# Feed-forward border of a one-core perceiver block: codes of h by two ScalarE additions, a W2 rounding moved behind the row maximum, four tiles turned early

## What is computed

```python
def _linear8bit(x, W, b):
    col_max = jnp.max(jnp.abs(x), axis=...)      # per column
    outlier = col_max > 3.0
    x_in = jnp.where(outlier, 0.0, x)
    x_out = jnp.where(outlier, x, 0.0)
    y = _ste_quant_rows(x_in) @ _ste_quant_rows(W).T
    return y + x_out @ W.T + b
h = _linear8bit(x, W1, b1)        # 256 x 4096
return _linear8bit(h, W2, b2)     # 256 x 1024
```

## Time and profile before

| | us |
|---|---|
| median of three executions | 937.74 (936.55 to 938.53) |
| profiled execution, device time | 937.01 |
| its span, first to last instruction | 934.9 |
| W1 stage's last matmul starts | 794.70 |
| W2 stage's first matmul starts | 803.87 |

### The profile page before, as it was taken

How to read it: one execution, slowest core, us unless ns; L and a number is a source line. 1 busy time by engine, 2 the same in 40 slices (tenths; PEclk the granted TensorE clock), 3 DMA queues, 4 the chain that set the end, 5 groups by cost and what they waited for, 6 DMA issues and landing times.

```text
span 934.9 us, 19043 instructions
## 1 busy us (share of the span) xinstructions
PE 897.1 (96%) x6856; PEld 820.6 (88%) x6856; DVE 702.4 (75%) x1124; ACT 614.1 (66%) x1060; POOL 488.2 (52%) x334
## 2 busy tenths in 40 slices
PE   7999999999999999999999999998899999799997
PEld 6997888888887889999999999986789999699997
DVE  6446666768546568888888888987988889988864
ACT  5424444565536478888888888885777878466662
POOL 0220000145444798686877868772377666266673
PEclk9999999999999999999999999999999999899999
DMA  8566766778763978656556565546135242224221
GB/s 320 191 206 232 290 224 250 277 271 308 278 189 113 271 224 271 199 183 183 182 176 215 172 193 169 195 168 215 46 136 181 97 172 94 87 91 180 90 90 46
DMA packets 80696, 174.82 MB, mean 187 GB/s; under 512 B 7632, under 2 KB 57584, under 8 KB 78064
## 3 DMA queue, kind: packets, MB, share of 16 engines
q1 hardware_dynamic: 79920, 173.63, 54.1%
q10 hardware_dynamic: 704, 0.23, 0.1%
HBM read 161.51 MB, written 11.53 MB: 185 GB/s over the span
## 4 chain that ended last, share of the span: by engine, by line
PE 73%; DVE 7%; issue 3%; ACT 3%; POOL 3%; DMA 2%; DVEq 0%; SPq 0%; ACTq 0%; POOLq 0%
PE bank L51 17%; PE bank L53 17%; PE bank L52 17%; PE bank L1408 4%; PE bank L1409 3%; PE bank L549 3%; PE bank L1379 3%; PE bank L1821 2%; PE bank L2051 2%; PE bank L1424 2%; POOL W_all L2287 1%; DMA ring<-in_L_attn_Wq_rope_dram 1%; ACT ring L1870 1%; DVE hT L1942 1%; POOL wl L1003 1%
## 5 line engine op out<-in xcount | busy, mean ns | idle before, releaser
L1003 POOL TENSOR_TENSOR wl<-ring,wh 128x1024 fp32r<-128x1024 f32 x68 | 161.6, 2395 | 0.0
L51 PE MATMUL bank<-act_all,W_all 128*128 128x256 f32 (+1 forms) x512 | 155.5, 304 | 3.0 <-POOL W_all L2287 2.0
L51 PE MATMUL bank<-act_all,wh 128*128 128x256 f32 x512 | 145.3, 284 | 1.8 <-POOL wl L1003 1.4
L53 PE MATMUL bank<-act_all,W_all 128*128 128x256 f32 (+1 forms) x512 | 145.4, 284 | 0.0
L52 PE MATMUL bank<-act_all,wh 128*128 128x256 f32 x512 | 144.7, 283 | 0.0
L53 PE MATMUL bank<-act_all,wl 128*128 128x256 f32 x512 | 144.3, 282 | 0.0
L513 POOL TENSOR_TENSOR xa_WT_l<-ring,xa_WT_h 128x1024 fp32r<-128x1024 f32 x16 | 43.5, 2741 | 176.6 <-ACT xa_WT_h L508 166.7
L1616 DVE TENSOR_TENSOR pl<-bank,ph 128x512 f16<-128x512 f32 x128 | 88.1, 688 | 47.1 <-ACT ph L1555 44.3
L2287 POOL TENSOR_TENSOR W_all<-rnd,W_all 128x512 fp32r<-128x512 f32 x72 | 92.1, 1289 | 54.5 <-ACT W_all L2176 54.4
L1000 POOL CAST wh<-ring 128x1024 fp32r<-128x1024 f32 x68 | 68.7, 1040 | 71.8 <-PE bank L53 66.0
L51 PEld LDWEIGHTS bank<-act_all,W_all 128*128 128x128 f32 x512 | 97.8, 191 | 4.4 <-POOL W_all L2287 2.6
(11 more groups left out here) (272 smaller groups left out, 2601.1 us busy)
## 6 DMA issues: line engine op xcount, KB each, us to landing
ring<-in_ctx_dram SPq DMA_DIRECT2D x16, 2048.0 KB, 7.9
ring<-in_L_attn_Wq_rope_dram SPq DMA_DIRECT2D x32, 1024.0 KB, 6.3
ring<-in_L_ffn_W_dram SPq DMA_DIRECT2D x14, 2048.0 KB, 7.6
panel<-in_L_ffn_W_dram SPq DMA_DIRECT2D x48, 512.0 KB, 4.3
w1p<-in_L_ffn_W_dram SPq DMA_DIRECT2D x16, 512.0 KB, 4.3
ring<-in_L_xattn_Wq_dram SPq DMA_DIRECT2D x2, 2048.0 KB, 12.8
ring<-in_L_xattn_Wk_dram SPq DMA_DIRECT2D x2, 2048.0 KB, 7.9
ring<-in_L_attn_Wo_dram SPq DMA_DIRECT2D x4, 1024.0 KB, 5.2
```

The lines of the kernel that those rows point to most:

```text
L51: pe.matmul(out, lh, rh, start=start, stop=False, skip_group_check=True)
L53: return pe.matmul(out, ll, rh, start=False, stop=stop, skip_group_check=True)
L1003: pool.tensor_tensor(half_of(l, i), half_of(r, i), f32(half_of(h, i)), ALU.subtract).then_inc(w_lo, 1)
```

## The change

- **Codes of h.** `codes` on DVE goes. ACT adds `mag2` to the scaled tile in place (`shifted_h`), then makes the high part by adding `-mag2` (`unmag2`, made once by ACT). DVE's `low_h` becomes a three-operand instruction that subtracts `mag2` and the high part. `shifted_h` stands in the even steps, `high_h` moves to the odd ones.
- **W2 rounding.** The rounding of tile 7 of the first W2 chunk, in the W1 stage's last step, moves behind the last `rows`; its high part on ACT moves too. Its low part is waited for only at k = 7 of step 0.
- **Turns.** Tiles 0 to 3 of chunk 1 are turned before step 0: 0 to 2 ahead of the row maximum's turn, 3 behind it. Step 0 then turns tiles 4 to 7 at k = 4 to 7, and step 1 none at k = 0 to 3. DVE rounds, and ACT takes the high part of, all eight tiles of chunk 1 in step 0.
- **PSUM.** The first two `scaled` read the inverse factors from the bank; the copy comes behind them. `clear(5)` moves into step 0.
- **Warm matmuls.** 5, 2 and 4 matmuls on zeros are put between PE's border steps.

```diff
@@ ffn2_tensor
-                pe.wait_ge(h_scaled, CH + NF)
-                for a in (6, 7):
-                    clear(a)
-                pe.wait_ge(r_max, NF + 1)
-                turn_rowmax(pe, runmax)
-                spread_factors(pe, 1)
-                pe.wait_ge(sx_copied, 2)
-                clear(4)
-                pe.wait_ge(q2_chain, 3)
-                clear(5)
-                pe.wait_ge(b_ready, 4 + (NW1 + 1) * KT)
-                pe.wait_ge(b_lo, 4 + (NW1 + 1) * KT)
-                pe.wait_ge(t_ready, (NW1 + 2) * CH)
...
                 def turn(c1, b, k):
                     pe.wait_ge(j_rnd, c1 * KT + (k + 1))
...
-                        if k < KT - LAG:
-                            if not first:
+                        if first == 0 and k >= KT - LAG:
+                            turn(1, 1, k)
+                        elif k < KT - LAG:
+                            if first is None:
                                 turn(c, b, k + LAG)
...
+                        if first == 0 and k == 0:
+                            pe.wait_ge(b_lo, 4 + (NW1 + 1) * KT - 1)
+                        elif first == 0 and k == KT - 1:
+                            pe.wait_ge(b_lo, 4 + (NW1 + 1) * KT)
...
+                            if first == 0 and k == 0 and j == 2:
+                                pe.wait_ge(q2_chain, 5)
+                                clear(5)
...
+                def warm(count):
+
+                    for _ in range(count):
+                        clear(7)
+
+                pe.wait_ge(h_scaled, CH + NF - 1)
+                clear(6)
+                pe.wait_ge(t_ready, (NW1 + 2) * CH)
+                for k in range(3):
+                    pe.wait_ge(b_ready, 4 + NW1 * KT + (4 + k + 1))
+                    turn(1, 1, k)
+                pe.wait_ge(h_scaled, CH + NF)
+                warm(5)
+                pe.wait_ge(r_max, NF + 1)
+                turn_rowmax(pe, runmax)
+                pe.wait_ge(b_ready, 4 + (NW1 + 1) * KT)
+                turn(1, 1, 3)
+                warm(2)
+                spread_factors(pe, 1)
+                pe.wait_ge(sx_copied, 2)
+                clear(4)
+                warm(4)
@@ ffn2_scalar
+                def shifted_h(nq, k, count=4):
+
+                    n = nq * KT + k
+                    tile = hT[:, ds(n, 1), :].rearrange("p a q -> p (a q)")
+                    act.wait_ge(q2_chain, n + count)
+                    act.activation(tile, tile, ACT.Identity, bias=mag2[:, ds(n, 1)]).then_inc(q2_b, 1)
...
-                                   hT[:, ds(n, 1), :].rearrange("p a q -> p (a q)"), ACT.Copy).then_inc(q2_hi, 1)
+                                   hT[:, ds(n, 1), :].rearrange("p a q -> p (a q)"), ACT.Identity,
+                                   bias=unmag2[:, ds(n, 1)]).then_inc(q2_hi, 1)
...
+                act.wait_ge(hm, (NW1 - 1) * 3 + 3 * CH)
+                act.activation(unmag2[:, :], mag2[:, :], ACT.Copy, scale=-1.0).then_inc(unmag_ready, 1)
+                act.wait_ge(b_ready, 4 + (NW1 + 1) * KT)
+                act.activation(W_h[0][:, KT - 1, :], rnd[(KT - 1) % 4][:, :], ACT.Copy).then_inc(b_hi, 1)
                 copy_factor(act, 1, sx2)
-                for k in range(KT):
-                    high_h(0, k)
...
+                for k in range(KT + 1):
+                    if k < KT:
+                        shifted_h(0, k, 3 if k < 2 else 4)
+                    if k >= 1:
+                        high_h(0, k - 1)
...
+                        if more and b == 1:
+                            high_h(nq + 1, k)
+                        if first == 0:
+                            high(1, k)
+                        elif k < KT - LAG:
+                            if first is None:
                                 high(c, k + LAG)
                         elif ahead:
                             high(c + 1, k + LAG - KT)
-                        if more:
-                            high_h(nq + 1, k)
+                        if more and b == 0:
+                            shifted_h(nq + 1, k)
                             for j in EVEN_AT[k]:
                                 scale_rows(c + 2, 0, n1 + 1, j)
@@ ffn2_vector
-                copy_inverse(dve, link, 1)
-                dve.wait_ge(b_lo, 4 + (NW1 + 1) * KT)
...
-                    dve.tensor_scalar(tile(hT, n), tile(hT, n), m, m, ALU.add, ALU.subtract).then_inc(q2_b, 1)
...
-                    dve.tensor_tensor(tile(hq_l, n), tile(hT, n), f32(tile(hq_h, n)), ALU.subtract).then_inc(q2_lo, 1)
+                    dve.scalar_tensor_tensor(out=tile(hq_l, n), in0=tile(hT, n), scalar=mag2[:, ds(n, 1)],
+                                             in1=f32(tile(hq_h, n)), op0=ALU.subtract, op1=ALU.subtract).then_inc(q2_lo, 1)
...
+                dve.wait_ge(row_spread, 2)
+                for k in range(2):
+                    scaled(k, bank[5][:, 0:T])
+                dve.tensor_copy(rsx[:, :], bank[5][:, 0:T]).then_inc(q2_chain, 1)
+                dve.wait_ge(q2_chain, 5)
+                for k in range(2, KT + 2):
                     if k < KT:
-                        scaled(k)
...
+                        scaled(k, rsx[:, :])
+                    low_h(k - 2)
+                dve.wait_ge(b_lo, 4 + (NW1 + 1) * KT)
...
+                        if first == 0:
+                            rounded(1, k, 0)
...
-                            scaled(nq * KT + (KT + k))
-                            codes(nq * KT + (KT + k))
+                            scaled(nq * KT + (KT + k), rsx[:, :])
@@ the W1 stage's last step: ACT, then DVE
-                            high(c + 1, 1 - b, k)
+                            if not (end and k == KT - 1):
+                                high(c + 1, 1 - b, k)
...
-                            rounded(c + 1, k, mag)
+                            if not (end and k == KT - 1):
+                                rounded(c + 1, k, mag)
...
+                        if end:
+                            rounded(c + 1, KT - 1, mag)
```

More of the change, by code:

```diff
@@ L1822, in turn, with step @@
                     last.then_inc(j_ready, 1)
-                def step(c, b, nq, ahead, first=False):
+                def step(c, b, nq, ahead, first=None):
                     for k in range(KT):
-                        if k < KT - LAG:
-                            if not first:
+                        if first == 0 and k >= KT - LAG:
+                            turn(1, 1, k)
+                        elif k < KT - LAG:
+                            if first is None:
                                 turn(c, b, k + LAG)
@@ L1855, in rows_back @@
                     last.then_inc(y_turned, 1)
-                step(0, 0, 0, True, first=True)
-                step(1, 1, 0, True)
+                def warm(count):
[18 more added lines that the diff above has]
+                warm(4)
+                step(0, 0, 0, True, first=0)
+                step(1, 1, 0, True, first=1)
                 with pe.Fori(1, NQ - 1) as i:
@@ L1907, in step @@
                             scale_rows(c + 1, 0, n1, k + 1)
[L1909 to L1910 removed]
+                step(0, 0, USE_W2, 0, True, first=0)
+                step(1, 1, USE_W2 + 1, 0, True, first=1)
                 with act.Fori(1, NQ - 1) as i:
                     for b in range(2):
[L1913 removed]
+                        step(i * 2 + b, b, i + (USE_W2 + b), i, True)
                 step(NCH - 2, 0, USE_W2 + NQ - 1, None, False)
@@ L1958, in rounded, with step @@
                     dve.tensor_scalar(rnd[k % 4][:, :], bank[k % 4][:, :], m, m, ALU.add, ALU.subtract).then_inc(j_rnd, 1)
-                for k in range(KT + 2):
-                    if k < KT:
-                        scaled(k)
-                    if 1 <= k < KT + 1:
-                        codes(k - 1)
-                    if k >= 2:
-                        low_h(k - 2)
-                def step(c, b, nq, ahead, more, first=False):
+                dve.wait_ge(row_spread, 2)
[4 more added lines that the diff above has]
+                for k in range(2, KT + 2):
+                    if k < KT:
+                        scaled(k, rsx[:, :])
+                    low_h(k - 2)
+                dve.wait_ge(b_lo, 4 + (NW1 + 1) * KT)
+                def step(c, b, nq, ahead, more, first=None):
                     for k in range(KT):
-                        if k < KT - LAG:
-                            if not first:
+                        if first == 0:
+                            rounded(1, k, 0)
+                        elif k < KT - LAG:
+                            if first is None:
                                 rounded(c, k + LAG, nq)
@@ L2184, in biased, with step @@
                         act.activation(tile, tile, ACT.Identity, bias=b1c[:, ds(n, 1)])
-                    def step(c, b, n2, inverse, first=False, tiles=TILES_AT):
+                    def step(c, b, n2, inverse, first=False, tiles=TILES_AT, end=False):
                         act.wait_ge(hp_ready, c * CH + CH)
```

(5 more changed lines are left out.)

27 lines of the change are left out of this document (9 added, 18 removed).

## The result

The changed kernel took 932.44 us, median of six runs (930.82 to 935.19), the kernel before 938.0 beside it: ratio 0.9939, 95% interval [0.9924, 0.9954]. That is 5.6 us faster. The forecast was 935.2 with a range of 932.0 to 939.2. The profiled execution took 932.16, its span is 930.1 (before 934.9), so 4.8 us of the gain can be looked for in the two traces.

The account below looks back on a forecast made before the run. PE, busy 96%, was taken as the bound, so gains come only where it waits or does needless work. Gains of 0.9 + 1.6 = 2.5 from profiled 937.0 give 934.5; median 0.7 above, 935.2; range 932.0 to 939.2.

Parts of the forecast that it names:

- The border: Between the last W1 and first W2 matmul: spread factors readable 0.95 us later; bounds 0.25 and 2.0 later.
- R: Time at the border when the spread factors can be read: 801.19 before, forecast 802.15 after.
- the zero matmul at 0.25: At the border, each matmul on zeros was costed at 0.25 us, five at 1.25.
- The bound of 2.0 later: Border's slow bound: count raised only after the moved rounding has ended, or transposes at half clock.
- Steps 0 and 1: Start of W2, up to the turn of chunk 2's tile 0: 827.15 instead of 828.04, 0.9 us earlier.
- last rounding R + 18.5: DVE's last rounding of step 0 starts 18.5 us after the spread factors can be read.
- the turn at R + 25.0: Chunk 2's tile 0 is turned in step 1, 25.0 us after the spread factors can be read.
- the 1.5 per pair: Step 0 on DVE: each `rounded` and `scaled` pair takes 1.5 us, about every second `scaled` held by POOL.
- Steps 2 to 5: W2 loop: each of two pairs of steps gives 0.8 us, 1.6 in all; bounds 2.9 won, 2.6 lost.
- w = 0.6: ACT's waits per pair of steps 2 to 5, taken as 0.6 us, so PE stands 0.9.
- Rival 2: ACT becomes the bound in W2's steps: w stays 2.75, four steps lose 2.6, total 940.1; chance 0.11.
- Rival 3: PE's clock falls in step 1 after standing 3 us: some 16 matmuls cost 1.5 more, 936.7; chance 0.12.

Follow-up runs that it names:

- the fifth experiment: The changed kernel with the codes of h back on DVE and `high_h` back in the even steps, other edits kept: 941.27 us, ratio 1.0035.

## Why the prediction was right, and where it was not

**The total** was right in its direction and range for a reason of which four fifths were not in it, and that is luck. The forecast won 2.5 us by the edits; they won about 1.1, less than the 1.9 that the forecast called the least difference to be told from none. With the tile's place undone the time was 937.35, also in the range and 2.15 above the 935.2, as the changed kernel is 2.8 below it. The other 4.5 came from the line that allocates `unmag2`, which the prediction didn't cost at all: it took a new small tile for nothing. No row of before shows that cost, since it is in each matmul's distance to the next, and nothing in the kernel before tells that this distance could be shorter.

**The border.** The mechanism on PE was right: the count comes just behind the last `runmax`'s start, PE's turns stand behind it and ahead of the row maximum's. On DVE, one of two terms was right: the `runmax` ahead of the last one takes 0.48 now, not the 1.27 that it took beside POOL's low part. The other failed: tile 3 of `hT` was to start 0.25 earlier, and it starts 0.97 behind the last W1 matmul, where it was 0.72, since DVE is busy until then with the `runmax` of the tile before. The last `runmax` starts 3.22 behind that matmul, not 2.7. From that `runmax` to R the steps give 802.15 - 797.4 = 4.75; measured 4.78 where the clock stayed up, 6.15 in the changed kernel's profile. The term that failed is the zero matmul at 0.25: five took 2.3 at half clock, 1.05 more, and the turn and its spread the rest. So R came 2.9 later against the last W1 matmul: 0.95 as forecast, 1.4 for the most part by the clock, 0.5 on DVE. The bound of 2.0 later had half clock for the transposes alone and was overrun by 0.9. Some of that is the profile of before, whose border was short: from the last `runmax` to R it took 2.77, but 3.30 in all four of its shifted forms.

PE waited 3.01 for L1966, a semaphore instruction of DVE with nothing to wait for itself. It ran at 793.6, behind the semaphore instructions of the last `runmax` (L2366, 793.4) and of the moved rounding (L2344, 793.5), but 0.26 ahead of the start of that rounding (793.86), which stands directly ahead of it in DVE's order. The Trainium skill's Perfetto Trace Analysis (Sequencer Loop) has engine instructions pushed into a queue, while the sequencer itself starts a control instruction. The trace agrees for the rounding, which waited only for its engine; the last `runmax`, whose wait was met late, was not passed.

**Steps 0 and 1.** First rounding at R + 8.0 as said, 8.06 measured; last rounding R + 18.5, measured 818.22, R + 18.6; the turn at R + 25.0, measured R + 25.05, and 25.05 to 25.10 in every kernel with these steps. The first W2 matmul at R + 2.3 was 2.5. These are the best terms of the forecast, but the 1.5 per pair is right only as a mean: `scaled` was to take 0.41 or 1.53 by turns, and it took 0.42, 1.34 and then 0.78 to 0.96 each time. What was wrong is what they were held against. Before's profile has the turn at R + 26.85; four kernels with the same code and other places have it at R + 25.73 to R + 25.75. The 1.1 is one instruction, the `scaled` of 1.53 in the earlier trace rows. In the kernel with the 256-byte tile, DVE's timeline has the same instruction as

```profile
822.83 0.42 DVE L1943 TENSOR_TENSOR hT<-hT,rows_q 128x256 f32<-128x256 f32 x1
```

and POOL's has its low parts as

```profile
822.78 2.91 POOL L1926 TENSOR_TENSOR W_all<-rnd,W_all 128x512 fp32r<-128x512 f32 x2 [2.25 <-ACT W_all L1877]
```

Each time POOL's instruction starts 0.05 ahead; once DVE's was held, once not. The Trainium skill's SBUF — State Buffer (SBUF: two separate sides) has the shared port pair as an exclusive lock, held by whichever starts first for the whole instruction. That fits the two lengths; the profile's starts, 0.05 apart, don't tell which came first. Where DVE's took 0.42, POOL's two took 2.90 to 2.92, and 2.73 where it took 1.53; this is as if POOL had waited instead, but no run shows it directly. So the true gain of these steps is 0.7 less what the border loses, where I had 0.9 after it.

**Steps 2 to 5.** Predicted 1.6, measured 2.35: the four distances at k = 4 make 10.81 before and 8.40 after, less 4 x 1.860 and 4 x 1.846. The other kernels without the edits make 11.06 to 11.24, the others with the edits 8.47 to 8.76. The term w = 0.6 was too large: PE stands 0.5 per pair, not 0.9, which leaves 0.2 for w. Rival 2 (ACT the bound) had no support.

**Rival 3**, chance 0.12, happened in the profiled execution: the clock fell behind the 2.87 us wait and cost 1.6 (1.5 forecast). It also happened in two more of the kernels with this wait, and behind the 7 us wait of the fifth experiment, and not in the one without the border's zeros.

Put together by typical values: 0.7 from the steps, 2.35 from the loop, less 0.9 to 2.3 at the border (last W1 matmul to R 8.0 to 9.4, against 7.1 in the middle of the five kernels without the edits, which took 6.5 to 8.0) and less up to 1.6 of clock: from 2.1 to -0.9, and 1.1 measured. The sum is too loose to check the 1.1 closely.

## What to carry to other kernels

Before costing a change, look at what its allocations move: an unused tile of the same size, and the change with its tile put last, separate the edit from the addresses in two runs. Hold a forecast against several executions of the old kernel where one instruction with two possible lengths lies on the path. And a semaphore that another engine waits for belongs ahead of the work that it doesn't depend on, above all where that engine runs in order.

## What the hardware showed that was not expected

- A tile's start in SBUF changes the rate of matmuls that wait for nothing: 1.846 against 1.860 for twelve and a turn, 75.89 to 76.83 for 64 matmuls of L1379 with what lies between them; over this kernel 4.65 us, 0.5%. A shift by 256 bytes changed nothing, 64, 96 and 128 did, each stage in its own way.
- The granted clock at one and the same place differs between profiles of kernels whose code is the same up to there: the five zero matmuls took 2.48 in one and 1.40 in another. A wait of 2.87 was followed by a granted clock of 0.63 in one kernel and of 1.00 in another, which differ in the border's five zeros only.
- An operation of DVE with two SBUF inputs that starts 0.05 behind one of POOL's took 1.53 in one profile and 0.42 in the four of the shifted kernels.
